# A one-core GNN and FFN kernel: the carried row of the segment sums is taken in another place of ScalarE's and VectorE's order, and x rows turn in another PSUM bank

## The reference

```python
edge_index = stack([src, dst])
x = x + gnn(layernorm(x), edge_index, W, att_src, att_dst, bias, ln_gamma, ln_beta)
x = x + ffn(layernorm(x)[None], Wr, br, W1, b1, W2, b2, gamma, beta)[0]

def gnn(x, edge_index, ...):        # H = 4 heads of C = 64; loops are added once more
    h = (x @ W).reshape(n, H, C)
    alpha = leaky_relu(a_src[src] + a_dst[dst], 0.2)          # a_* = <h, att_*>
    alpha = exp(alpha - segment_max(alpha, dst)[dst])
    alpha = alpha / (segment_sum(alpha, dst)[dst] + 1e-16)
    out = segment_sum(alpha[:, :, None] * h[src], dst).reshape(n, H * C) + bias
    return relu(layer_norm(out, ln_gamma, ln_beta))
```

## Time and profile before

| what | value |
|---|---|
| median of 3 runs | 3,504.13 us (3,502.38 to 3,505.12) |
| profiled execution, its own time | 3,474.59 us |
| profiled execution, span | 3,472.8 us |
| busy: PE, DVE, ACT, POOL | 2,494.7, 2,261.4, 1,741.6, 1,606.7 us |
| the 119 steps | about 224 to 2,725 us of the span |
| FFN phase | from about 2,800 us on |

### The profile page before, as it was taken

How to read it: one execution, slowest core, us unless ns; L and a number is a source line. 1 busy time by engine, 2 the same in 40 slices (tenths; PEclk the granted TensorE clock), 3 DMA queues, 4 the chain that set the end, 5 groups by cost and what they waited for, 6 DMA issues and landing times. The chain is left out here.

```text
span 3472.8 us, 66576 instructions
## 1 busy us (share of the span) xinstructions
PE 2494.7 (72%) x13162; PEld 1809.5 (52%) x13162; DVE 2261.4 (65%) x9525; ACT 1741.6 (50%) x5715; POOL 1606.7 (46%) x1689
## 2 busy tenths in 40 slices
PE   7746666766666766666666666666666699999998
PEld 6534445555554555454444444444444466666666
DVE  5446676766766667676666666666666655655555
ACT  4436666666665666665655555555555422222221
POOL 5465555655655656555666666666666000000000
PEclk9858888887778888888888888888888799999999
DMA  8944444444444444444444444444445201111110
GB/s 282 325 130 129 130 136 133 134 134 131 133 131 129 135 135 134 131 133 131 133 130 130 132 131 131 132 133 133 132 130 128 68 31 37 39 39 38 37 36 33
DMA packets 238971, 415.86 MB, mean 120 GB/s; under 512 B 67998, under 2 KB 153502, under 8 KB 238878
## 3 DMA queue, kind: packets, MB, share of 16 engines
q0 software_dynamic: 80064, 229.34, 24.9%
q1 hardware_dynamic: 157462, 184.01, 16.3%
q10 hardware_dynamic: 1351, 1.62, 0.2%
HBM read 361.68 MB, written 53.13 MB: 119 GB/s over the span
## 5 line engine op out<-in xcount | busy, mean ns | idle before, releaser
L781 POOL DMA_INDIRECT rows<-table,idx x1594 | 1526.3, 958 | 1008.6 <-issue 404.0
L874 PE MATMUL bank<-msg,oh 128*128 128x260 f32 x3332 | 984.7, 451 | 115.4 <-issue 99.4
L874 PEld LDWEIGHTS bank<-msg,oh 128*128 128x128 f32 x3332 | 750.5, 230 | 287.8 <-issue 134.1
L1105 ACT ACTIVATE msg<-rows,we 128x65 f32<-128x65 f32 x1904 | 478.6, 333 | 0.4
L1406 DVE TENSOR_TENSOR msg<-rows,bank 128x520 f32<-128x520 f32 x595 | 382.3, 677 | 0.6 <-DVEq L111 0.3
L992 PE MATMUL bank<-rows,msg 128*128 128x256 f32 x1536 | 340.6, 378 | 0.0
L979 PE MATMUL bank<-rows 128*128 128x512 f32 x768 | 335.8, 595 | 2.6 <-DMA rows<-in_L_ffn_W 2.6
L1098 ACT ACTIVATE oh_b<-bank 128x896 bf16<-128x896 bf16 x238 | 205.3, 914 | 244.3 <-remote 226.4
L922 PE MATMUL bank<-ident_b,ohT 128*128 128x128 bf16 x1666 | 178.8, 289 | 199.0 <-DVE acc L1553 52.0
L1241 ACT ACTIVATE msg<-bank,b_sb 128x512 f32<-128x512 f32 (+1 forms) x200 | 134.4, 679 | 364.4 <-PE bank L979 346.7
L992 PEld LDWEIGHTS bank<-rows,msg 128*128 128x128 f32 x1536 | 288.4, 189 | 51.4 <-issue 10.3
(11 more groups left out here) (223 smaller groups left out, 4108.8 us busy)
## 6 DMA issues: line engine op xcount, KB each, us to landing
dst_b<-dst SPq DMA_DIRECT2D x121, 448.0 KB
rows<-table,idx POOLq DMA_INDIRECT x1594
tab_w<-table SPq DMA_DIRECT2D x120, 134.5 KB
x_w<-in_x_rows SPq DMA_DIRECT2D x120, 128.0 KB
x_mid<-x_o SPq DMA_DIRECT2D x119, 128.0 KB
table<-msg SPq DMA_DIRECT2D x50, 269.0 KB
rows<-x_mid SPq DMA_DIRECT2D x26, 512.0 KB, 3.9
msg<-in_x_rows SPq DMA_DIRECT2D x51, 256.0 KB
```

The lines of the kernel that those rows point to most:

```text
L781: pool.indirect_dma_start(rows[:, slot, t, :], None, table, bass.IndirectOffsetOnAxis(ap=idx[slot][:, t:t + 1], axis=0), bounds_check=None ...
L874: mm = pe.matmul(psA, oh[:, of, t, :], msg[:, of, t, :], start=(t == 0), stop=(t == TILES - 1))
L1105: ins = act.activation(head_cols(msg[:, s, t, :])[:, h, :], head_cols(rows[:, at.slot(), t, 0:HC1])[:, h, :], ACT.Copy, scale=we[:, t, h:h ...
```

## The change

ScalarE's copy of the carried row (`carry`) moves from ahead of `msgs0` to behind `oh*`. `acc` and `oh*` come right after `msgs`; then `carry`, `rexp` and `carried`. VectorE's five operations on the carried row leave the messages and the work on the next chunk's segments: `r_t` now stands behind `MTILE*`, ahead of the first half of the one-hots, and waits there for ScalarE's copy; `r_sc`, `r_mn`, `r_d1` and `r_d` stand between the one-hots' halves. The first half of the turned x rows is written to bank 3, at columns 352 to 479, in place of bank 5: PE no longer waits for ScalarE's `carry` before it turns x rows, and waits for ScalarE's `xT` before `expand*` (which writes bank 3) in place of before its own `carry` product.

```diff
         dve2 = Ticks(sem("dve2"), """
-            ... st_m msg0 mv_m msg1 msg2 msg3 r_t msg4
-            wcur^ r_sc newseg^ r_mn node^ r_d1 r_d pen^ NODE_V* RUNMAX^ NOHAS* LASTMAX^ MTILE* ohT0^ MNODE* AD* MAXSELF* ohT^ ZN*
+            ... st_m msg0 mv_m msg1 msg2 msg3 msg4
+            wcur^ newseg^ node^ pen^ NODE_V* RUNMAX^ NOHAS* LASTMAX^ MTILE* r_t ohT0^ r_sc MNODE* r_mn AD* r_d1 r_d MAXSELF* ohT^ ZN*
-        act2: oh_b* we we_act carry msgs0 asrc^ msgs rexp acc carried oh* xrow xT ...
+        act2: oh_b* we we_act msgs0 asrc^ msgs acc oh* carry rexp carried xrow xT ...
-        psXT = [bank[5][:, 320:320 + P], bank[6][:, 328:328 + P]]
+        psXT = [bank[3][:, 352:352 + P], bank[6][:, 328:328 + P]]
...
                 if to_turn:
                     dve2.wait(pe, MSGS[-1], at)
-                    act2.wait(pe, "carry", at)
                     act2.wait(pe, "xT", at, -1)
...
                 if ahead:
+                    if to_turn:
+                        act2.wait(pe, "xT", at)
                     dve2.wait(pe, "LO*", at)
...
                     act2.wait(pe, "carry", at)
-                    act2.wait(pe, "xT", at)
                     pe2.mark("carry", pe.matmul(psC, sel[...], acc[:, :], start=True, stop=True))
...
-                if before:
-                    pe2.wait(act, "carry", at, -1)
-                    act2.mark("carry", act.activation(carry[:, :], psC, ACT.Copy))
...
                 if prev:
-                    dve2.wait(act, "r_d", at)
-                    act2.mark("rexp", act.activation(r_f[:, :], r_d[:, :], ACT.Exp))
                     pe2.wait(act, "agg", at)
                     dve2.wait(act, "biased3", at, -1)
                     pe2.wait(act, "carry", at, -1)
                     act2.mark("acc", act.activation(acc[:, 0:HC1], psA, ACT.Copy))
+                if ahead:
+                    pe2.wait(act, "agg", at)
+                    act2.mark("oh*", copy_one_hots(oh[:, q, :, :]))
+                if before:
+                    pe2.wait(act, "carry", at, -1)
+                    act2.mark("carry", act.activation(carry[:, :], psC, ACT.Copy))
+                if prev:
+                    dve2.wait(act, "r_d", at)
+                    act2.mark("rexp", act.activation(r_f[:, :], r_d[:, :], ACT.Exp))
                     act2.wait(act, "rexp", at)
                     act2.wait(act, "carry", at)
                     for h in range(H): ... scale=r_f[:, h:h + 1])
                     act2.mark("carried", ins)
-                if ahead:
-                    pe2.wait(act, "agg", at)
-                    act2.mark("oh*", copy_one_hots(oh[:, q, :, :]))
...
+                if prev:
+                    act2.wait(dve, "carry", at)
+                mark(prev, "r_t", ...)
                 mark(far, "ohT0^", lambda: one_hots(0))
+                done("r_t")
+                mark(prev, "r_sc", ...)
                 mark(ahead, "MNODE*", ...)
+                done("r_sc")
+                mark(prev, "r_mn", ...)
                 mark(ahead, "AD*", ...)
+                done("r_mn")
+                mark(prev, "r_d1", ...)
+                mark(prev, "r_d", ...)
                 mark(ahead, "MAXSELF*", ...)
                 mark(far, "ohT^", lambda: one_hots(1))
```

More of the change, by code:

```diff
@@ L362, in build @@
         dve2 = Ticks(sem("dve2"), """
-            EDGE_V self_z ZE self_l LE SEL* D MASK* DMIN self_d LAST_HI* LAST_R* LAST_MID* MPEN* LAST_LO* st_m msg0 mv_m msg1 msg2 msg3 r_t msg4
-            wcur^ r_sc newseg^ r_mn node^ r_d1 r_d pen^ NODE_V* RUNMAX^ NOHAS* LASTMAX^ MTILE* ohT0^ MNODE* AD* MAXSELF* ohT^ ZN*
+            EDGE_V self_z ZE self_l LE SEL* D MASK* DMIN self_d LAST_HI* LAST_R* LAST_MID* MPEN* LAST_LO* st_m msg0 mv_m msg1 msg2 msg3 msg4
+            wcur^ newseg^ node^ pen^ NODE_V* RUNMAX^ NOHAS* LASTMAX^ MTILE* r_t ohT0^ r_sc MNODE* r_mn AD* r_d1 r_d MAXSELF* ohT^ ZN*
             accshift SHIFT* mergedshift HI* REST* MID* merged0 merged1 LO* merged2 merged3 den rden
@@ L367, in build @@
         FIRST_ROW = 6
-        act2 = Ticks(sem("act2"), """oh_b* we we_act carry msgs0 asrc^ msgs rexp acc carried oh* xrow xT wself selfm ln2 y2 lhs ln1 y1 xln xrstd""", 6)
+        act2 = Ticks(sem("act2"), """oh_b* we we_act msgs0 asrc^ msgs acc oh* carry rexp carried xrow xT wself selfm ln2 y2 lhs ln1 y1 xln xrstd""", 6)
         pe2 = Ticks(sem("pe2"), "nodemax* agg lT^ xrow xT lastT^ turned^ expand* half router carry", 6)
@@ L1122, in step @@
                     act2.skip(act, ["we", "we_act"], at)
-                if before:
-                    pe2.wait(act, "carry", at, -1)
-                    act2.mark("carry", act.activation(carry[:, :], psC, ACT.Copy))
-                else:
-                    act2.skip(act, ["carry"], at)
                 if own:
@@ L1151, in step @@
                     act2.mark("acc", act.activation(acc[:, 0:HC1], psA, ACT.Copy))
+                else:
+                    act2.skip(act, ["acc"], at)
+                if ahead:
+                    pe2.wait(act, "agg", at)
+                    act2.mark("oh*", copy_one_hots(oh[:, q, :, :]))
+                else:
+                    act2.skip(act, ["oh*"], at)
+                if before:
+                    pe2.wait(act, "carry", at, -1)
+                    act2.mark("carry", act.activation(carry[:, :], psC, ACT.Copy))
+                else:
+                    act2.skip(act, ["carry"], at)
+                if prev:
+                    dve2.wait(act, "r_d", at)
+                    act2.mark("rexp", act.activation(r_f[:, :], r_d[:, :], ACT.Exp))
                     act2.wait(act, "rexp", at)
@@ L1158, in step @@
                 else:
-                    act2.skip(act, ["rexp", "acc", "carried"], at)
-                if ahead:
-                    pe2.wait(act, "agg", at)
-                    act2.mark("oh*", copy_one_hots(oh[:, q, :, :]))
-                else:
-                    act2.skip(act, ["oh*"], at)
+                    act2.skip(act, ["rexp", "carried"], at)
                 if to_row:
@@ L1480, in step @@
                 mark(before, "mv_m", lambda: dve.bn_aggr(x_o[:, s, D:D + 2], st2[:, :]))
-                for name in MSGS[1:4]:
+                for name in MSGS[1:]:
                     message(name)
-                if prev:
-                    act2.wait(dve, "carry", at)
-                mark(prev, "r_t", lambda: dve.tensor_scalar(r_t[:, :], carry[:, HAS:HAS + 1], BIG, -BIG, ALU.mult, ALU.add))
-                message(MSGS[4])
                 mark(far, "wcur^", lambda: dve.tensor_copy(wcur[:, s, :], w_tab[:, bass.ds(at.number(2), 2)]))
-                done("r_t")
-                mark(prev, "r_sc", lambda: dve.tensor_scalar(r_sc, carry[:, SHIFT:HAS], r_t[:, 0:1], None, ALU.add))
                 if far:
@@ L1493, in step @@
                     newseg[:, s, 1:P], dst_s[:, s, 1:P], dst_s[:, s, 0:P - 1], ALU.not_equal))
-                done("r_sc")
-                mark(prev, "r_mn", lambda: dve.tensor_tensor(r_mn, r_sc, adsh[0:1, q4, H:], ALU.max))
                 done("wcur^")
                 mark(far, "node^", lambda: dve.tensor_tensor(node[:, s:s + 1], iota_col[:, :], wcur[:, s, 0:1], ALU.add))
-                done("r_mn")
-                mark(prev, "r_d1", lambda: dve.tensor_tensor(r_d[:, 0:H], r_sc, r_mn, ALU.subtract))
-                mark(prev, "r_d", lambda: dve.tensor_tensor(r_d[:, H:], adsh[0:1, q4, H:], r_mn, ALU.subtract))
                 if beside:
@@ L1520, in step @@
                     mtile[:, :, :], node_v[:, :, 1:R5], over(nohas[:, :], H), ALU.add))
+                if prev:
+                    act2.wait(dve, "carry", at)
+                mark(prev, "r_t", lambda: dve.tensor_scalar(r_t[:, :], carry[:, HAS:HAS + 1], BIG, -BIG, ALU.mult, ALU.add))
                 if far:
@@ L1525, in step @@
                 mark(far, "ohT0^", lambda: one_hots(0))
+                done("r_t")
+                mark(prev, "r_sc", lambda: dve.tensor_scalar(r_sc, carry[:, SHIFT:HAS], r_t[:, 0:1], None, ALU.add))
                 done("MTILE*")
@@ L1528, in step @@
                     mnode[:, :], mtile[:, :, :].rearrange("p t h -> p h t"), X, ALU.max))
+                done("r_sc")
+                mark(prev, "r_mn", lambda: dve.tensor_tensor(r_mn, r_sc, adsh[0:1, q4, H:], ALU.max))
                 if ahead:
```

2 lines of the change are left out of this document (added).

## The result

The changed kernel takes 3558.53 us (3554.01 to 3567.52, 4 runs) against 3503.87 us of the kernel before beside it (4 runs): a ratio of 1.0159 [1.0138, 1.018]. It is 1.6% slower where 1.9% faster was forecast. The profiled execution has 3,567.5 us, with a span of 3,565.7 against 3,472.8, so 92.9 us more. That is more than the 55 us between the medians: the profiled execution of the kernel before lies 29.5 us under its median, and that of the changed kernel is the slowest of its four.

A forecast was written before the change was run, and what follows sets the result against it. POOL was taken to pace the step by gathers, spaces and two stops; 0.95 us of a 1.2 us excess in the second stop, over 68 early steps, gave 65 us less: 3,504.1 to 3,439 us, range 3,408 to 3,520.

The forecast's parts named there:

- Part 1: ScalarE's copy leaves the messages' front: earlier `asrc^` shortens POOL's stop before the seventh gather, at most 82.8 us over all.
- Part 2: DVE's five operations leave the messages, no gain given, and return among the one-hots at 0.3 to 0.5 us in sum.
- Part 3: DVE's `r_t` waits 1.2 us for the copy ahead of `ohT0^`; with Part 2, `ohT^` 1.6 us later against `node_v`.
- Part 4: ScalarE's second half: `oh*` ends 1.05 us earlier against `acc`; PE's turning 4.3 us behind `node_v`, 0.3 later.
- Part 5: X rows in bank 3: `expand*` waits for `xT`, 5.7 us behind `node_v`, 0.2 later, only in steps with x rows.
- What is on the path: Delays of DVE (1.6 us) and PE (0.2 to 0.3) weighed against POOL's next stop; later steps given 0.
- the slack: Margin of about 2 us between when `lT^` can be done and when POOL can use it for the seventh gather.
- Rival (c): Slower: DVE's new wait before `ohT0^` costs more than the slack; 37 us more, 3,541 us; chance 0.22.
- the 1.68 us one: DVE's idle stretch before `st` in the second half; two more like it, 2.2 us together, were assumed in Rival (c).
- Rival (b): The stall moves: ScalarE stands still whatever comes next, messages start as late as the copy did; 0 us, 3,504; chance 0.16.

The follow-up runs named there:

- k1: Kernel before with ScalarE's copy moved behind `asrc^` and DVE's five operations on the carried row ahead of `NODE_V*`: ratio 0.9943 on a 3,476 us chip.
- k18: Same edit to the kernel before as k1, on another chip: ratio 0.9948 at 3,472 us.
- k3: Kernel before with only the x rows' bank and its waits changed: ratio 0.9978 on a 3,476 us chip.
- k15: The kernel before, unedited, rerun for its trace on a 3,506 us chip: ratio 0.9996.
- k17: Same edit to the changed kernel as k4, on another chip: ratio 1.009 to the kernel before at 3,506 us.
- k4: Changed kernel with ScalarE's copy alone put back ahead of `msgs0`: ratio 0.9929 to the kernel before on a 3,476 us chip.
- k5: Kernel before with k1's edit, `oh*` ahead of `rexp` and `carried`, and x rows in bank 3: ratio 0.9999 at 2,959 us.
- k11: Changed kernel with ScalarE's copy between `acc` and `oh*`: ratio 0.9998 to the kernel before on a 2,964 us chip.
- k13: Same edit to the kernel before as k5, on another chip: ratio 0.9973 at 2,964 us.

## Why the prediction was wrong

**Part 1, the copy leaves the front: right in its mechanism, over-sized in its yield.** `asrc^` starts 2.20 us behind the weights in every step (some 2.5 forecast). By itself that gives 0.3 to 0.4 us per early step (k1, k18) and not 0.95. In the changed kernel none of it arrives, as the weights come 2.4 us later behind the first gather. The reading it rests on, that an increment of PE is seen late, fits the trace's own records (above); they show the same of DVE's increments, which the prediction did not take into account.

**Part 2, five operations among the one-hots: right.** The two halves of `ohT` are 1.31 us apart instead of 0.94: 0.37, where 0.3 to 0.5 was taken.

**Part 3, DVE's wait: right in size, wrong in what it costs.** DVE stands 0.92 us in the steps where it waits (25.8 over 28, 28.6 over 31), 1.2 forecast; `ohT^` is 3.2 us behind `node_v` in early steps and 3.6 in later ones, 3.6 forecast.

**Part 4, PE's turning: right in early steps, too small in later ones.** It starts 4.0 (early) and 4.4 us (later) behind `node_v`, 4.3 forecast. But the 4.0 us from which the "0.3 later" was worked out is that of an early step; in later steps the turning stood 3.1 us behind `node_v`, so there it is 1.25 us later. That PE would be idle for 3.6 us there and come back at half the clock was in no part of the sum.

**Part 5, the bank:** `expand*` is 6.7 us behind `node_v` in early steps, where 5.7 was worked out; alone (k3) the bank gains 0.2%.

**The step that failed is "What is on the path".** It gave the 1.6 us of DVE the bounds 0 and 1.6, "still inside the slack", and the later steps 0. The slack was measured rightly (1.96 us). But the delay was not the only thing to set against it: DVE's idle of 0.09 us before `st` became 3.40, the chain behind `st` took the place of the short one behind the edge maxima, the weights came 2.6 us later behind the first gather, and the eight sums, at the low clock, ended 1.9 us later behind the weights. **Rival (c) came about**: the weights late behind the first gather, the slack passed, the second stop 3.3 to 3.5 us. It took 3.8 us for the weights' lateness (2.4 to 2.6 measured) and 37 us in all (55 measured), and it placed them in the early steps, where a quarter of the excess of the two traces is (20 of 79 us), and a tenth beside the trace of k15. Its 2.2 us for two more stretches "like the 1.68 us one" are less than twice 1.68, which is 3.4. What it set against itself, that "a later DVE meets fewer" idle stretches, is the opposite of what the steps show: between `node_v` and `st` DVE now stands 5.1 us in a later step, 0.05 before, and 4.1 us in an early one, 1.7 before. In the early steps the idle before `st` did fall (1.66 to 0.55 us), but only since DVE is now held ahead of `rden`, 2.3 us per step, where it was not before.

Rival (b) is out: with the copy away ScalarE's messages start at once (`asrc^` at 2.20 us in every step), so its standing still belonged to the wait for PE's product. That wait was met 5.8 us after the product in the earlier trace rows, 4.7 us on average. The Trainium skill's 26.3 ns per increment, cited in the prediction from "TensorE: Matmul & The Clock Gate", section "The cost: per-tile semaphore tail", tells how the increments of packed tiles add up behind one another; for this wait no run here bears it out. What makes the increments late stays open, as does why k17 loses on the 3,506 us chip what k4 gains on the 3,476 us one; the difference stands in the table (0.6 us more idle before `st`, 0.8 us more of PE idle), not its cause.

## What to carry to other kernels

A slack has to be held against everything that hangs behind it, and against where the waiting engine will stand when the next burst of gathers ends: here an idle just before the last link cost little, and the same idle ahead of `st` cost the chain behind it. When the data for TensorE come later in the cycle it idles longer, and here the sums that followed ran at half clock; compare the mean of the first matmuls after the idle, not only busy shares. Where a view says "remote", look up in the program what the instruction waits for: here it was the engine's own last operation. And an order that gains 0.7% on one chip can lose 0.9% on another: a change of this size is to be timed on more than one.

## What the runs showed of the hardware that was not expected

- The kernel before takes 3,472 to 3,506 us on some chips and 2,959 and 2,964 us on others. On the fast ones the steps are 16.5 and 17.5 to 17.7 us (k5, k11, k13), POOL has few stops, and DVE is 77 to 78% busy.
- After 3.5 us without a matmul PE's eight sums had a granted clock of 0.50 and took 3.67 us; after 1.0 us 1.00 and 1.92 us.
- Near the end of a batch of gathers DVE and PE stand still together and go on at the same moment (2021.65 in the timeline, beside POOL's own stop of 2.61 us). DVE waits for nothing but its own semaphore there, whose increments are recorded up to 4.2 us behind the end of its last operation; in the traces on chips near 2,960 us they are never recorded more than 0.08 us behind.
